# Other orders of the calls on every engine, and other PSUM banks, in the transformer blocks of a one-core kernel

## The reference

```python
x = x + gate_a * (attention(modulate(ln(x))) @ W_proj + b_proj)      # self attention, 16 heads of 16
x = x + (attention(ln(x) @ W_qc, context kv) @ W_cproj + b_cproj)    # cross attention, 77 keys
x = x + gate_m * (gelu(modulate(ln(x)) @ W_mlp1 + b1) @ W_mlp2 + b2) # 256 -> 1024 -> 256
```

## Time and profile before

| | |
|---|---|
| median of 3 runs | 2812.12 us |
| the profiled execution | 2806.85 us |
| its span, first to last instruction | 2805.0 us |
| mean granted TensorE clock | 0.971 of full |
| blocks | from about 720 us to the end |

### The profile page before, as it was taken

The page is one execution under the profiler, slowest core; times in us unless marked ns, Lnnn a source line. Parts: engine busy times, 40 slices in busy tenths (PEclk is TensorE's granted clock), DMA queues, the critical chain, the costliest instruction groups (busy, mean ns, idle before and its releaser), DMA issues.

```text
span 2805.0 us, 63074 instructions
## 1 busy us (share of the span) xinstructions
PE 2674.4 (95%) x24004; PEld 2291.8 (82%) x24004; DVE 1819.4 (65%) x3703; ACT 1533.4 (55%) x2637; POOL 943.0 (34%) x954
## 2 busy tenths in 40 slices
PE   7999999999479999999999999999999999999997
PEld 6999999999357887887787788788788788888876
DVE  2444444443456877787777777778777677777753
ACT  3444444443235656666565566666566566666652
POOL 3334334333102333333333333333333233233323
PEclk8999999999678999999999999999999999999998
DMA  6243433310535545444555554544555554455531
GB/s 177 93 130 103 138 118 111 97 52 9 158 69 106 120 101 112 116 110 101 134 123 146 126 113 99 119 119 102 121 124 125 154 113 112 101 120 115 106 77 31
DMA packets 326715, 308.69 MB, mean 110 GB/s; under 512 B 130320, under 2 KB 252608, under 8 KB 326416
## 3 DMA queue, kind: packets, MB, share of 16 engines
q1 hardware_dynamic: 316336, 279.10, 41.6%
q10 hardware_dynamic: 10080, 25.57, 2.6%
HBM read 118.89 MB, written 51.93 MB: 61 GB/s over the span
## 4 chain that ended last, share of the span: by engine, by line
PE 60%; issue 3%; DMA 3%; DVE 3%; SPq 3%; ACT 2%; POOL 1%; POOLq 0%; ACTq 0%; DVEq 0%
PE gbank L2625 8%; PE obank L2465 8%; PE obank L2550 7%; PE gbank L2465 7%; PE score L2516 4%; PE score L2530 4%; PE gbank L2472 4%; PE obank L2596 3%; PE obank L2472 3%; PE obank L2480 2%; PE obank L2565 2%; PE gbank L2456 2%; PE score L2579 2%; ACT p_f L1955 2%; PE gbank L2565 2%
## 5 line engine op out<-in xcount | busy, mean ns | idle before, releaser
L1955 ACT ACTIVATE p_f<-score 128x1024 f32<-128x1024 f32 (+1 forms) x576 | 563.6, 1021 | 331.4 <-PE score L2579 249.4
L2226 DVE TENSOR_REDUCE m_a<-score 128x4 f32<-128x1024 f32 x384 | 461.9, 1216 | 56.0 <-PE score L2516 49.7
L1905 POOL TENSOR_TENSOR h_c<-h_f,h_c 128x512 fp32r<-128x512 f32 x192 | 250.5, 1306 | 366.4 <-DVE h_c L2292 366.4
L2625 PE MATMUL gbank<-w_down,h_c 128*128 128x256 f32 x2304 | 341.0, 295 | 2.3 <-POOL h_c L1905 2.2
L2625 PEld LDWEIGHTS gbank<-w_down,h_c 128*128 128x128 f32 x2304 | 293.8, 192 | 28.4 <-issue 16.7
L1299 PE MATMUL m_ps<-m_comb,m_w 128*128 128x256 f32 x2304 | 297.6, 285 | 1.5 <-PEq L258 1.5
L1299 PEld LDWEIGHTS m_ps<-m_comb,m_w 128*128 128x128 f32 x2304 | 280.7, 188 | 5.6 <-issue 3.6
L2465 PE MATMUL obank<-xT_c,w_up 128*128 128x256 f32 x1728 | 238.8, 288 | 4.8 <-ACT h_f L1974 2.8
L2465 PEld LDWEIGHTS obank<-xT_c,w_up 128*128 128x128 f32 x1728 | 217.3, 192 | 7.4 <-ACT h_f L1974 3.0
L2530 PE MATMUL score<-q_cat,k_cat 50*128 50x256 f32 x1536 | 219.2, 323 | 3.6 <-ACT p_f L1955 3.2
L820 POOL TENSOR_TENSOR m_hhl<-m_hf,m_hhl 128x512 fp32r<-128x512 f32 x96 | 124.6, 1298 | 290.1 <-DVE m_hhl L1085 289.6
(11 more groups left out here) (291 smaller groups left out, 5461.0 us busy)
## 6 DMA issues: line engine op xcount, KB each, us to landing
k_cat<-k_hl SPq DMA_DIRECT2D x288, 128.0 KB, 3.8
q_cat<-q_hl SPq DMA_DIRECT2D x288, 128.0 KB, 4.1
qc_cat<-qc_hl SPq DMA_DIRECT2D x288, 128.0 KB, 3.2
split_L<-m_cut SPq DMA_DIRECT2D x36, 512.0 KB, 3.1
x_a<-x_after_L SPq DMA_DIRECT2D x48, 256.0 KB, 2.8
x_b<-x_after_L SPq DMA_DIRECT2D x48, 256.0 KB, 2.9
kc_cat<-cross_keys SPq DMA_DIRECT2D x96, 115.5 KB, 3.6
cross_keys<-m_kvk SPq DMA_DIRECT2D x162, 64.0 KB, 2.2
```

The source lines that it names most:

```text
L1905: e.tensor_tensor(h_c[:, 1, 2 * i:2 * i + 2, :], h_f[:, i % 2, :, :], h_c[:, 0, 2 * i:2 * i + 2, :].bitcast(F32), ALU.subtract).then_inc(S ...
L1955: e.activation(slot(phase, i)[0:n, :], score[i % 2].ap[0:n, :, :].rearrange("p h n -> p (h n)"), ACT.Exp, scale=SCALE).then_inc(ex.sem, 1)
L2226: e.tensor_reduce(m_a[:, :, i::NPAIR].rearrange("p t h -> p h t"), score[i % 2].ap[:, :, :].rearrange("p h (t k) -> p h t k", t=TT), AX.X, ...
L2625: mm = e.matmul(B_DOWN.ap[:, tt, :], h_c[:, xp, 2 * i + c, tt * P:(tt + 1) * P], W["down"][:, i, wp, c, :], start=(i + wp + xp + c == 0), ...
```

## The change

On each of the five engines the calls stand in another order in the loop. Some calls move into a neighbouring round, seen by another offset (`keys(n - 2)` is `keys(n - 3)`, all of the MLP on TensorE is one round later by number as the loop's first line has moved), and the loops have one round more or less. The four single banks are dealt out anew. No instruction is added or taken away and no function that a call names is changed. `exp_table`, `gelu_table` and `next_rest` keep their effect and are called for another n.

```diff
-        B_QK, B_QQ, B_RB, B_DOWN, B_OC, B_CXT, B_KMT, B_QXT, B_V, B_RA, B_T, B_XT, B_MT, B_KQ = (
-            g0, g1, o1, g1, o1, g0, g0, g0, o0, o1, g1, g1, g1, o1)
-        B_UP, B_KP = (o0, g0, o0, o0), (o1, g0)
+        B_T, B_QXT, B_XT, B_KQ, B_MT, B_QK, B_RB, B_QQ, B_OC, B_DOWN, B_KMT, B_V, B_CXT, B_RA = (
+            o1, g1, o1, o0, o1, g1, o1, o0, o0, g0, o0, o1, g1, g1)
+        B_UP, B_KP = (g0, g1, o1, o0), (o1, g1)
```

VectorE's loop, the part that the prediction speaks of most:

```diff
+                cross_max(n - 6, 2, 0)
+                cross_max(n - 6, 2, 1)
+                self_normed(n - 3)
+                cross_max(n - 6, 3, 0)
+                self_max(n - 4, 0)
+                cross_max(n - 6, 3, 1)
+                mlp_normed(n - 7)
+                cross_max_low(n - 6)
...
-                cross_max(n - 5, 1, 0)
-                self_normed(n - 2)
-                cross_max(n - 5, 1, 1)
-                cross_max(n - 5, 2, 0)
-                mlp_normed(n - 6)
-                cross_max(n - 5, 2, 1)
-                cross_max(n - 5, 3, 0)
-                cross_max(n - 5, 3, 1)
-                self_max(n - 3, 0)
-                cross_max_low(n - 5)
```

More of the change, by code:

```diff
@@ L2396, in _ @@
             selection_out()
[L2397 to L2404, removed]
+            for n in range(0, 56):
+                self_sum(n - 6)
+                cross_stats(n - 6)
+                self_max(n - 5, 4)
+                self_max(n - 5, 5)
+                cross_normed(n - 6)
+                self_max(n - 5, 6)
+                cross_x_low(n - 6)
+                self_max(n - 5, 7)
+                cross_recips(n - 7)
+                mlp_h_high(n - 8, 0)
+                self_max_low(n - 5)
+                cross_queries_low(n - 6)
+                mlp_h_high(n - 8, 1)
+                cross_heads_normed(n - 7)
+                keys_low(n - 4)
+                mlp_h_high(n - 8, 2)
+                cross_sum(n - 7)
+                self_stats(n - 3)
+                mlp_stats(n - 7)
+                cross_max(n - 6, 0, 0)
+                cross_max(n - 6, 0, 1)
+                cross_max(n - 6, 1, 0)
+                cross_max(n - 6, 1, 1)
+                mlp_h_high(n - 8, 3)
+                cross_max(n - 6, 2, 0)
[6 more added lines that the diff above has]
+                cross_max_low(n - 6)
+                self_max(n - 4, 1)
+                self_max(n - 4, 2)
+                self_recips(n - 5)
@@ L2725, in cross_projected @@
                 by_token(B_OC, 1, oT_b, W["oc"]).then_inc(S["B_op"].sem, 1)
-            for n in range(0, 54):
+            for n in range(0, 55):
+                self_max_rows(n - 4)
+                keys(n - 3)
+                up(n - 7, 2)
+                up(n - 7, 3)
+                cross_recips_spread(n - 6)
+                down(n - 7, 0)
+                self_scores(n - 4, 0)
+                self_scores(n - 4, 1)
+                cross_projected(n - 6)
+                down(n - 7, 1)
+                self_scores(n - 4, 2)
+                self_scores(n - 4, 3)
+                self_values(n - 4, 0)
+                cross_plain(n - 5, 0, 0)
+                self_scores(n - 4, 4)
+                cross_plain(n - 5, 0, 1)
+                cross_plain(n - 5, 1, 0)
+                cross_plain(n - 5, 1, 1)
+                self_scores(n - 4, 5)
+                self_scores(n - 4, 6)
+                cross_plain(n - 5, 2, 0)
+                cross_plain(n - 5, 2, 1)
+                self_values(n - 4, 1)
+                cross_plain(n - 5, 3, 0)
+                self_scores(n - 4, 7)
+                cross_plain(n - 5, 3, 1)
+                self_plain(n - 3, 0)
+                self_values(n - 4, 2)
+                self_values(n - 4, 3)
+                self_plain(n - 3, 1)
+                self_plain(n - 3, 2)
+                cross_max_rows(n - 5)
+                down(n - 7, 2)
+                self_turned(n - 2)
+                down(n - 7, 3)
+                down(n - 7, 4)
+                values(n - 3, 0)
+                values(n - 3, 1)
+                cross_scores(n - 5, 0)
+                self_plain(n - 3, 3)
+                mlp_turned(n - 6)
+                queries(n - 2)
+                down(n - 7, 5)
+                cross_scores(n - 5, 1)
+                cross_scores(n - 5, 2)
+                self_recips_spread(n - 4)
+                down(n - 7, 6)
+                down(n - 7, 7)
                 self_projected(n - 4)
+                cross_scores(n - 5, 3)
+                self_plain(n - 3, 4)
+                cross_values(n - 5, 0)
                 cross_values(n - 5, 1)
```

163 lines of the change are left out of this document (47 added, 116 removed).

## The result

| | before | after |
|---|---|---|
| median, same chip | 2812.02 us (4 runs) | 2849.37 us (4 runs, 2838.95 to 2870.62) |
| ratio, 95% interval | 1 | 1.0152 [1.0122, 1.0182] |
| profiled execution, its span | 2806.85, 2805.0 us | 2840.07, 2838.3 us |
| mean granted TensorE clock | 0.971 | 0.948 |

The change made the kernel 1.5% slower. The forecast was 2795 us within 2758 to 2830: wrong in sign and outside its range.

What follows compares the result with a forecast made beforehand. TensorE, busy for 95%, was taken as the bound. Per period -0.68 - 0.2 - 0.64 + 0.9 + 0.2 = -0.42 us; times 44 is -18, +3 at the ends is -15: forecast 2795 us, range 2758 to 2830.

Steps and rivals of the forecast that it cites:

- Fewer changes of kind: TensorE: 22 runs of one kind of matmul a round instead of 26, -0.68 us a period.
- halves side by side: TensorE: cross_plain calls of opposite array halves adjacent at three places could overlap, 0 to 0.4 us gained, 0.2 taken.
- the old waits: TensorE: three short waits, at self_values(2), cross_max_rows and for xn_b, go: -0.64 us a period.
- New wait 1: TensorE: self_values(2) waits for VectorE's cross_max(3,0) on bank o1, behind self_normed at about 1.75 us: +0.9 us a period.
- (b): Rival, slower: both self_normed halves wait behind GpSimd, the two new waits total 2.4 us; period 41.5, 2854 us, chance 0.18.
- New wait 2: TensorE: self_recips_spread waits for the reciprocals' transfers on SP's queue, +0.2 us a period, between 0 and 0.5.
- Layer-end loads: Weight loads at the two layer ends meet another small transfer: between -5 and +5 us for the program, taken as 0.
- Filling and emptying: Program's ends: emptying perhaps 8 us longer, last bias load ahead of the store -5; net +3 us, from -5 to +12.
- (a): Rival, full gain: self_normed meets a quiet GpSimd, self_values(2) doesn't wait; period 39.3, 2757 us, chance 0.20.
- (c): Rival, no change: two thin covers fail by 0.2 us each, period within 0.1 us; 2810 us, chance 0.17.
- The signs that the text had asked for: New profile: period 40.2 us, 22 kinds a round, about 0.9 us gap before self values, none ahead of cross_max_rows.

Runs made afterwards that it cites:

- e1: Changed kernel with self_normed moved behind cross_max(3,1) on VectorE: 2842.12 us, ratio 1.0111 to the kernel before.
- e5: Changed kernel with self_normed behind cross_max(3,1) on VectorE and down(1) behind cross_plain(0,1) on TensorE: 2797.59 us, ratio 0.9966 to the kernel before.
- b2: Kernel before with down(2) moved on TensorE from ahead of self_values(2) to behind self_values(3): 2866.09 us, ratio 1.0194.
- b1: Kernel before with self_normed moved right ahead of cross_max(3,0) on VectorE, TensorE's order untouched: 2816.17 us, ratio 1.0022.
- e3: Changed kernel with next_up_high and next_down, loads of the next layer's weights, moved later on ScalarE: 2854.7 us, ratio 1.0140 to the kernel before.
- e9: Kernel of e5 with next_up_low and next_up_high moved some 3 us earlier on ScalarE: 2796.78 us, ratio 0.9953 to the kernel before.

## Why the prediction was wrong

*Fewer changes of kind, halves side by side, the old waits: -1.52 us a round.* Right as a sum. Without both new waits it gives 39.1 us a round, and e1 shows 39.15 to 39.2, with a wait of 0.2 us in it that the text doesn't have; so the three terms came to about 1.7 us. Their shares weren't measured apart. (Two readings in the text are a little off, without weight in the sum: VectorE was busy for 158.24 us and not 158.3, and of the 0.24 us at the old self_values(2) the table of waits has 0.16 as wait.)

*New wait 1, +0.9.* Right in place and cause, mis-sized: 1.30 us (after, timeline). The term rested on self_normed at 1.75 us; it took 2.09, because both halves met a GpSimd instruction, which the text had kept for rival (b). e1 removes it and the round falls by 1.3 us.

*New wait 2, +0.2.* Missing. The table of waits has self_recips_spread's only in three rounds:

```profile
PE obank L2550 <- DVE m_b L2236: 31.3, 25, 1.3
...
PE gbank L2503 <- DMA rcat_a<-r_a: 1.7, 3, 1.0
```

*A wait that the text doesn't have:* 0.2 us ahead of cross_plain(1, 0), in 41 rounds. The text laid out cross_plain's calls side by side as a gain only.

The sum of these steps is thus 40.2 predicted and 40.5 measured, still a small gain.

*The step that failed is one that the text doesn't have.* It counted TensorE's calls at durations taken from the earlier trace rows, all at a granted clock of 1.00, and took the clock as given. The new order draws together what stood apart, which won the changes of kind and at the same time made 11.3 us without full-array work, with a wait of 0.2 us inside; there the clock falls in 14 of the 39 ordinary rounds, some +30 us where the sum has nothing, and in two of the longest. That the order sets the falls is shown by the pair e1 and e5 (25 falls to 6 with one call moved, 2842.12 to 2797.59 us), and from the other side by b2. That the gap of 1.3 us is not needed is shown by e1, that a gap of up to 0.8 us at self_values(2) isn't enough by b1. What in the order does it is not shown: the edit that took the falls away put full-array work into the stretch and removed the 0.2 us wait at once.

The Trainium skill (TensorE: Matmul & The Clock Gate, Part 1) says that the gate sets its level by how busy TensorE has been recently. The busy time of the trace doesn't bear that out here: 3.70 of 3.90 us ahead of the fall at 1735.9.

*Layer-end loads, 0 within -5 and +5.* For TensorE's waits near enough: other small transfers were met (6.68 and 7.90 us in the chain), and its waits in the four longest rounds went from 15.6 to 17.7 us. Yet these rounds grew by 18.5 us. Most of the rest fits the falls of the clock, 44.4 us low against 17.1, which is the failed step once more. No run took the two apart, and e3 and e9, which moved the loads, won nothing clear of the noise.

*Filling and emptying, +3.* The emptying was longer by 6.9 us, as expected in sign. The filling was shorter by 15.5 us, which nothing in the text foresaw and no run took apart.

*The rivals.* (b) named 2854 us, but its round of 41.5 us is not what is seen and its two waits came to 1.3 us, not 2.4: that its time was nearly met is luck, since another mechanism made it. (a)'s round was reached in e1, its time nowhere. (c) is out. The signs that the text had asked for, 40.2 us and a gap of 0.9 us, were nearly there (40.49 and 1.30), and the kernel was slower all the same.

## What to carry to other kernels

When an order is changed on a bound TensorE, list what the new stretches are made of, and the short waits inside them, and not only their length: this order, which gathered small row-tiled and narrow matmuls and put a short wait between them, lost more through the granted clock than it won in changes of kind. A busy share near 100% hides it; compare the granted clock, and the number of matmuls done in equal stretches, before the waits. If a regression has two causes, remove each alone and both together: here each alone left the kernel slower than before (1.0111 and 1.0080), and the two together made it faster (0.9966).

## What the runs showed of the hardware

With one core at work the granted clock falls from 2.4 to 1.2 GHz in the midst of nearly unbroken work of TensorE (3.70 of 3.90 us busy ahead of one fall), for 3.4 to 17.1 us at a time. The place of six full-array matmuls (0.97 us in e5) goes with most of these falls: with down(1) behind cross_plain(0, 1) there are 6, 0.9 us earlier 19, 1.2 us later 21. Whether it is these matmuls or the 0.2 us wait that they cover isn't shown.

A change of kind costs TensorE 0.06 to 0.1 us at each end of a run. That four runs fewer were worth what this makes isn't shown by itself; it held in a sum of three terms, to within 0.2 us a round.

Transfers of 16 KB took 6.68 and 7.90 us in the chain just behind a weight load issued from another engine's queue. The second of them, s_b, took 3.16 us in the chain at 1458.52, away from these loads:

```profile
1458.52 3.16 DMA s_b<-u_b
```
